# A gated cross-attention block on one core: a new opening for the first batch's mask, queries and keys

## The chip, the cores and the metric

The kernel runs on one core of one Trainium2 chip. The metric is the time of one execution in device microseconds (us). Engines: TensorE (PE) multiplies matrices, VectorE (DVE), ScalarE (ACT) and GpSimd (POOL) do elementwise work, SyncE (SP) issues most transfers. Transfers issued by SP stand in one queue, those issued by ACT in another; sixteen DMA engines serve both.

## What is computed

```python
def attention(query, key, value, mask, ...):      # 16 heads of 8, D = 128
    q = query @ qw.T + qb; k = key @ kw.T + kb; v = value @ vw.T + vb
    scores = einsum('bhqd,bhkd->bhqk', split(q) * DH ** -0.5, split(k))
    scores = where(mask[:, None] == 0, -1e9, scores)
    return merge(softmax(scores) @ split(v)) @ ow.T + ob

x = x + tanh(g_xattn[0]) * attention(layernorm(x), ctx, ctx, mask, ...)   # x: 16 x 56 x 128, ctx: 16 x 1500 x 128
x = x + tanh(g_ffn[0]) * mixture_of_experts(layernorm(x), ...)            # 8 experts, top 2, one shared
```

The mask has 16 x 56 x 1500 entries.

## The kernel before

One batch is one unit of work, and units are pipelined by hand: in unit k the program makes K of batch k+2, scores, their maxima and V of batch k+1, and transposed scores, exponentials and the product with V of batch k. Three buffers (`NB`) rotate for the context (`ctxT`), the score operand (`keys`) and V. Each engine has its own instruction stream, written in the order in which it runs; streams wait for each other on semaphores. `units` runs a unit function for k from -1 (on SP from -2) to 15, and calls a function of the table that it is given ahead of a unit. What stands ahead of `units` in each stream is the opening.

The score operand `keys[:, buffer, pair, :]` has 121 rows that one matmul contracts for a pair of heads: rows 0 to 63 are K as a high and a low fp16 part (rows r, r+4, ... for r = 0 to 3), rows 64 to 120 are the mask's additive term, one row per query, with a row of ones at row 96 (`ONEROW`), against which the running maximum is subtracted. The mask rows are the same for all eight pairs of heads. VectorE makes them once (`mask_add`, two halves of 750 keys on rows 0 to 63 and 64 to 127), and the sync queue copies them eight times into `keys` ("placing"), in four transfers a batch: 32 and 24 rows for either half, skipping the row of ones, which one transfer writes into all buffers at the start. K is placed in four transfers too, each 16 x 8 runs of 1500 values.

The opening loads x, the first context and the constants, normalises x (`dve_layer_norm`), turns it on TensorE (`turn_ln`, two halves), makes K of batch 0 (`pe_k`, three chunks) and all queries (`make_queries`, two halves), splits each into fp16 parts, and places them. `pe_any` and `dve_any` find the queries with no valid key. `pool_queries` makes the query operand `qrs` of a batch. The second stage of the opening (`load_second`, `load_third`) loads contexts 1 and 2, the next masks, places the queries of the later batches and loads the output weights (`ow_rows`, `o_bias`). Ahead of unit 0 TensorE folds V's bias into the output bias (`fold_bias`), which waits for these.

## Time and profile before

| | |
|---|---|
| time, median of 3 runs | 525.68 us (525.66 to 526.95) |
| profiled execution: its own time | 525.51 us |
| profiled execution: span | 523.7 us |
| PE busy | 473.9 us, 90% of the span |
| DVE busy | 399.2 us, 76% |
| ACT busy | 329.6 us, 63% |
| POOL busy | 160.5 us, 31% |
| moved by the DMA engines | 72.82 MB, 139 GB/s over the span |

The span is the time between the first and the last instruction that the profiler saw. The busy shares are means over the whole span: the opening (to about 57 us), the units of the loop (23 us each) and the mixture of experts at the end have different limits, so a stage is read by its own rows.

### The profile page before, as it was taken

The numbers are of one execution on the slowest core, as the hardware profiler recorded it, in microseconds if no ns is written. First come the engines' busy times: TensorE is split into PE (matmuls) and PEld (weight loads), VectorE is DVE, ScalarE is ACT, GpSimd is POOL, SyncE is SP. The second block draws the span as 40 slices with busy tenths as digits, with TensorE's granted clock in tenths as the row PEclk, the third lists the DMA queues.
The fourth block names the chain that finished last, engine by engine and source line by source line (L and its number), as shares of the span: only waits on it lengthen the run. The fifth ranks groups of instructions, "written<-read, shape, count | busy, mean of one in ns | idle before, by whom it ended". The sixth has DMA issues, their size and how long they took to land.

```text
span 523.7 us, 15766 instructions
## 1 busy us (share of the span) xinstructions
PE 473.9 (90%) x6779; PEld 351.7 (67%) x6779; DVE 399.2 (76%) x784; ACT 329.6 (63%) x422; POOL 160.5 (31%) x142
## 2 busy tenths in 40 slices
PE   1547699999999999999999999999989989999993
PEld 0214377867778686777768677786868856777772
DVE  7339477877877887787788787778867768888776
ACT  2311366666676666667666666766665788877872
POOL 4034326061532606153351615335194200000000
PEclk9959799999999999999999999999999999999998
DMA  5899986996979688796969869684500300221001
GB/s 165 179 254 195 245 193 134 250 200 165 192 173 202 147 184 177 165 199 169 207 134 197 173 162 197 173 171 105 120 3 2 84 2 25 57 73 51 3 1 35
DMA packets 39805, 72.82 MB, mean 139 GB/s; under 512 B 4638, under 2 KB 26271, under 8 KB 39736
## 3 DMA queue, kind: packets, MB, share of 16 engines
q1 hardware_dynamic: 38456, 70.90, 60.6%
q8 instruction: 53, 0.87, 0.8%
q10 hardware_dynamic: 1280, 0.92, 0.7%
q14 instruction: 16, 0.13, 0.1%
HBM read 24.28 MB, written 0.46 MB: 47 GB/s over the span
## 4 chain that ended last, share of the span: by engine, by line
PE 78%; DVE 7%; DMA 5%; ACT 3%; issue 3%; SPq 1%; POOL 1%; ACTq 0%; DVEq 0%
PE ring L342 16%; PE pv L382 16%; PE st L363 11%; PE ring L324 8%; PE ring L286 7%; PE st L858 7%; PE ring L911 6%; DMA ctxT<-in_ctx 4%; DVE max_part L536 2%; ACT v_ext L469 2%; DMA ident_h<-in_c_ident_h 2%; PE pv L911 2%; SPq L268 1%; PE ring L307 1%; PE ring L350 1%
## 5 line engine op out<-in xcount | busy, mean ns | idle before, releaser
L536 DVE TENSOR_REDUCE max_part<-ring 112x1 f32<-112x512 f32 (+1 forms) x384 | 244.9, 675 | 73.4 <-PE ring L342 73.2
L489 ACT ACTIVATE probs<-st 128x896 f32<-128x896 f32 x192 | 172.5, 916 | 73.5 <-PE st L363 71.4
L342 PE MATMUL ring<-keys,qrs 121*112 121x512 f16 (+1 forms) x384 | 149.7, 391 | 6.8 <-DVE max_part L536 3.3
L363 PEld LDWEIGHTS st<-qrs,keys 121*128 121x128 f16 (+1 forms) x1536 | 97.2, 102 | 29.5 <-issue 8.9
L363 PE MATMUL st<-qrs,keys 121*128 121x112 f16 (+1 forms) x1536 | 106.7, 213 | 1.0 <-ACT qrs L478 1.0
L382 PE MATMUL pv<-probs,v_ext 128*32 128x168 f32 (+3 forms) x3072 | 93.6, 262 | 0.1
L382 PEld LDWEIGHTS pv<-probs,v_ext 128*32 128x32 f32 (+1 forms) x3072 | 73.1, 109 | 21.7 <-issue 11.3
L342 PEld LDWEIGHTS ring<-keys,qrs 121*112 121x112 f16 x384 | 49.9, 130 | 41.7 <-DVE max_part L536 17.7
L614 POOL TENSOR_TENSOR k_hi<-k_raw,zero 128x512 f16<-128x512 f32 (+1 forms) x45 | 45.8, 1018 | 86.7 <-ACT k_raw L457 86.7
L286 PE MATMUL ring<-ctxT,w_qkv 128*128 128x512 f32 (+1 forms) x94 | 53.6, 656 | 13.7 <-DMA ctxT<-in_ctx 13.7
L324 PE MATMUL ring<-w_qkv,ctxT 128*128 128x128 f32 (+1 forms) x384 | 60.0, 278 | 1.7 <-ACT v_ext L469 0.5
L324 PEld LDWEIGHTS ring<-w_qkv,ctxT 128*128 128x128 f32 (+1 forms) x384 | 56.3, 188 | 6.4 <-ACT v_ext L469 4.4
L457 ACT ACTIVATE k_raw<-ring,biases 128x512 f32<-128x512 f32 (+1 forms) x45 | 30.5, 677 | 42.5 <-PE ring L286 40.6
L886 DVE TENSOR_TENSOR keys<-probs,keys 128x896 f16<-128x896 f32 (+2 forms) x44 | 40.3, 919 | 17.6 <-ACT keys L879 17.3
L617 POOL TENSOR_TENSOR k_lo<-k_raw,k_hi 128x512 f16<-128x512 f32 (+1 forms) x45 | 51.2, 1138 | 3.5
L635 POOL TENSOR_TENSOR attn<-sums,recip 128x112 f32<-128x112 f32 x15 | 6.3, 421 | 142.0 <-DVE recip L565 132.2
L869 ACT ACTIVATE probs<-st,up_bias 128x896 f32<-128x896 f32 (+2 forms) x44 | 38.2, 869 | 16.6 <-PE st L858 16.3
L858 PE MATMUL st<-keys 128*128 128x512 f16 (+1 forms) x216 | 47.7, 353 | 0.7 <-ACT probs L869 0.7
L469 ACT ACTIVATE v_ext<-ring 128x512 f32<-128x512 f32 (+1 forms) x48 | 27.1, 565 | 26.7 <-PE ring L324 26.7
L911 PE MATMUL ring<-keys 128*128 128x128 f16 x612 | 41.5, 219 | 1.6 <-DVE keys L886 1.6
L911 PEld LDWEIGHTS ring<-keys 128*128 128x128 f16 x612 | 36.5, 98 | 9.2 <-DVE keys L886 2.9
L626 POOL TENSOR_TENSOR qrs<-queries,any_key 121x896 f16<-121x896 f16 x16 | 30.2, 1887 | 22.5 <-DMA queries<-probs 22.5
(122 smaller groups left out, 352.0 us busy)
## 6 DMA issues: line engine op xcount, KB each, us to landing
ctxT<-in_ctx SPq DMA_DIRECT2D x16, 750.0 KB, 6.2
keys<-mask_add SPq DMA_DIRECT2D x32, 375.0 KB
keys<-k_hi SPq DMA_DIRECT2D x32, 375.0 KB, 6.3
keys<-k_lo SPq DMA_DIRECT2D x32, 375.0 KB, 7.3
keys<-mask_add SPq DMA_DIRECT2D x32, 281.2 KB
mask_raw<-in_mask SPq DMA_DIRECT2D x15, 375.0 KB, 3.5
up_w<-in_up_w SPq DMA_DIRECT2D x9, 256.0 KB, 2.9
down_w<-in_down_w SPq DMA_DIRECT2D x9, 256.0 KB, 3.2
```

Of the source, the lines that this page charges most:

```text
L286: nc.tensor.matmul((first_k[c] if known(k, -1) else misc)[:, 0:width(c)], w_qkv[:, 1, :], ctxT[:, w, chunk(c)], start=True, stop=True).the ...
L324: mm = nc.tensor.matmul(misc[0:m, i * P:(i + 1) * P], ctxT[:, buf(b, 1), j * P:j * P + m], w_qkv[:, 2, :], start=True, stop=True)
L342: nc.tensor.matmul(ring[0:QW, m % 2, 0:width(c)], qrs[0:ROWS, w, p, :, :].rearrange("r h q -> r (h q)"), keys[0:ROWS, w, p, chunk(c)], sta ...
L363: mm = nc.tensor.matmul(st[0:m, j % 2, p // 4, QW * (p % 4):QW * (p % 4 + 1)], keys[0:ROWS, u, p, j * P:j * P + m], qrs[0:ROWS, u, p, :, : ...
L382: mm = nc.tensor.matmul(pv[rows, last * HG * S:last * HG * S + n * S], v_ext[0:m, u, j, VW * h:VW * h + CW], probs[0:m, j % 4, S * h:S * ( ...
L489: nc.scalar.activation(probs[0:m, j % 4, :].rearrange("p (h c) -> p h c", h=2), st[0:m, j % 2, :, 0:HQ // 2], ACT.Exp).then_inc(s["exps_do ...
L536: nc.vector.tensor_reduce(max_part[:, p, c:c + 1], ring[0:QW, m % 2, 0:width(c)], AX.X, ALU.max).then_inc(s["max_read"], 1)
L614: nc.gpsimd.tensor_tensor(k_hi[:, chunk(c)], k_raw[:, chunk(c)], zero[:, :].to_broadcast([P, width(c)]), ALU.add).then_inc(s["k_hi_made"], 1)
L617: nc.gpsimd.tensor_tensor(k_lo[:, chunk(c)], k_raw[:, chunk(c)], k_hi[:, chunk(c)], ALU.subtract).then_inc(s["k_lo_made"], 1)
L858: mm = nc.tensor.matmul(st[:, n % 2, h, 0:cols], split_w[e][:, 0, w, c * P:(c + 1) * P], xn_p[:, x, 4 * P * h:4 * P * h + cols], start=(i ...
L886: nc.vector.tensor_tensor(hid[:, n % HR, 1, cols], hid_raw[n % 3][:, cols], hid[:, n % HR, 0, cols], ALU.subtract).then_inc(s["hid_lo_done ...
L911: mm = nc.tensor.matmul(down_banks[e % 2][t // 4][:, P * (t % 4):P * (t % 4 + 1)], hid[:, n % HR, x, P * t:P * (t + 1)], split_w[e][:, 1, ...
```

## The change

The first batch's mask no longer goes through `mask_add` and the sync queue. It is loaded in the layout of the mask rows (`first_mask`, 64 rows of 1500, into a part of `keys` that is free so early), VectorE makes the rows of pair 0 in place, and VectorE (pairs 1 and 2, then 3 to 5) and ScalarE (pairs 6 and 7) copy them to the other pairs. The row of ones is now a row of the mask: its entry is 0 and its factor 1 (`mask_scale`, one factor per row, in place of the constant -32768), so that one transfer places 64 rows, two transfers a batch instead of four, and the transfer that wrote the ones is gone. TensorE turns both halves of x and makes the first queries ahead of K; the identity for the maxima (`ident_h`) is waited for later. The first queries are issued by SP instead of ACT, ahead of the first keys, which are split into buffer 2 of `keys` and placed in three chunks, each with a semaphore of its own. Context 1 and mask 1 are issued once the first mask has landed, context 2 behind the first keys; the later queries follow the placement of mask 1, and the output weights stand behind batch 1's keys. TensorE makes the first chunk of batch 1's K ahead of unit -1.

```diff
+        first_hi, first_lo = keys[:, NB - 1, 0, :], keys[:, NB - 1, 1, :]
+        first_mask = keys[MROW:P, NB - 1, 2:4, :].rearrange("r p k -> r (p k)").bitcast(I32)
...
+        def sp_place_mask(sp, b):
...
+            for h in range(2):
+                sp.dma_start(keys[MROW:P, w, :, h * HK:(h + 1) * HK],
+                             mask_add[MROW * h:MROW * (h + 1), :].unsqueeze(1)
+                             .to_broadcast([MROW, PAIRS, HK])).then_inc(mask_placed[w], 16)
...
-                for h in range(2):
-                    for r0, r1 in ((0, QSPLIT), (QSPLIT + 1, NR)):
-                        sp.dma_start(keys[MROW + r0:MROW + r1, w, :, h * HK:(h + 1) * HK],
...
+                for c in range(NCH) if known(k, -1) else ():
+                    sp.wait_ge(s["k_lo_made"], c + 1)
+                    for r in range(4):
+                        sp.dma_start(keys[r:MROW:4, w, :, chunk(c)], (first_lo if r % 2 else first_hi)[:, chunk(c)])                            .then_inc(first_placed[c], 16)
...
+                if known(k, 0):
+                    pe.wait_ge(s["rows_spread"], 2)
+                    pe.wait_ge(s["rows_copied"], 1)
+                    pe.wait_ge(first_placed[0], 64)
...
-            nc.vector.tensor_scalar(mask_add[:, :], mask_raw[:, :], 0.0, -BIG,
+            nc.vector.tensor_scalar(mask_add[:, :], mask_raw[:, :], 0.0, mask_scale,
...
-            sp.wait_ge(s["ones_set"], 2)
-            sp.dma_start(keys[ONEROW:ONEROW + 1, :, :, :].rearrange("r u p k -> r (u p) k"),
-                         ones_row[:, :].unsqueeze(1).to_broadcast([1, NB * PAIRS, NK])).then_inc(s["ones_placed"], 16)
 
             def load_second():
+                sp.wait_ge(s["mask_loaded"], 16)
                 sp_load_ctx(sp, 1, 1)
                 sp_load_mask(sp, 1)
+                sp.wait_ge(s["q_hi_done"], 1)
+                sp_place_first_queries(sp, 0)
+                sp.wait_ge(s["q_split"], 1)
+                sp_place_first_queries(sp, 1)
+
+            def load_next():
+                sp.wait_ge(s["q_made"], 2)
+                sp_load_ctx(sp, 2, 2)
+                sp_place_mask(sp, (-1, -1 % NB, -1 // NB))
                 sp.wait_ge(s["q_split"], 2)
...
+            def load_output():
+                for c in range(NCH):
+                    sp.wait_ge(first_placed[c], 64)
                 sp.dma_start(ow_rows[:, :, :], d["ow"]).then_inc(s["consts_loaded"], 16)
                 sp.dma_start(o_bias[:, :], d["ob"].unsqueeze(0)).then_inc(s["consts_loaded"], 16)
-
-            def load_third():
-                sp_load_ctx(sp, 2, 2)
...
-            units(sp, sp_unit, {-1: load_second, 0: load_third, 2: load_ffn}, first=-2)
+            units(sp, sp_unit, {-2: load_second, -1: load_next, 0: load_output, 2: load_ffn}, first=-2)
...
+            act.wait_ge(s["mask_ready"], 1)
+            nc.scalar.activation(keys[MROW:ROWS, 0, COPIED:PAIRS, :],
+                                 keys[MROW:ROWS, 0, 0:1, :].to_broadcast([NR, PAIRS - COPIED, NK]),
+                                 ACT.Copy).then_inc(s["rows_copied"], 1)
...
-            pe.wait_ge(s["weights_loaded"], 32)
+            pe.wait_ge(s["weights_loaded"], 16)
             pe.wait_ge(s["qkv_loaded"], 32)
             turn_ln(0)
-            pe_k(pe, FIRST, 0)
-            pe_k(pe, FIRST, 1)
+            turn_ln(1)
             make_queries(0)
-            pe_k(pe, FIRST, 2)
-            turn_ln(1)
+            for c in range(NCH):
+                pe_k(pe, FIRST, c)
             make_queries(1)
-            pe_any(pe, FIRST)
-
-            def await_ones():
-                pe.wait_ge(s["ones_placed"], 16)
+
+            def second_k():
+                pe_k(pe, (-1, -1 % NB, -1 // NB), 0)
+                pe_any(pe, FIRST)
+                pe.wait_ge(s["ident_loaded"], 16)
...
+            def spread_mask(pairs):
+
+                dve.wait_ge(s["mask_ready"], 1)
+                n = len(pairs)
+                nc.vector.tensor_copy(keys[MROW:ROWS, 0, pairs[0]:pairs[-1] + 1, :],
+                                      keys[MROW:ROWS, 0, 0:1, :].to_broadcast([NR, n, NK])).then_inc(s["rows_spread"], 1)
```

On SP, from the last two placements of the first keys on (`k_hi`, `k_lo`) to the placement of mask 1, before:

```order
L268 DMA keys<-k_hi 16x8x1500
L268 DMA keys<-k_lo 16x8x1500
L240 DMA ctxT<-in_ctx 128x1500
L245 DMA mask_raw<-in_mask 128x750
L990 DMA queries<-probs 16x8x784 [waits s_q_split]
L990 DMA queries<-probs 16x8x784 x3
L992 DMA ow_rows<-in_ow 128x256
L993 DMA o_bias<-in_ob 1x128
L245 DMA mask_raw<-in_mask 128x750 [waits s_mask_abs_done,s_mask_ready]
L263 DMA keys<-mask_add 32x8x750
L263 DMA keys<-mask_add 24x8x750
```

Before these stood the ones row and the first mask's four placements; behind them follow the second half of mask 1, batch 1's keys, and only then context 2 (`ctxT`). On SP after the change, behind the twelve placements of the first keys:

```order
L257 DMA ctxT<-in_ctx 128x1500 [waits s_q_made]
L262 DMA mask_raw<-in_mask 128x750 [waits s_mask_abs_done,s_mask_ready]
L276 DMA keys<-mask_add 64x8x750 x2
L1031 DMA queries<-probs 16x8x784 [waits s_q_split]
L1031 DMA queries<-probs 16x8x784 x3
L296 DMA keys<-k_hi 16x8x1500 [waits s_k_lo_made]
L296 DMA keys<-k_lo 16x8x1500
L296 DMA keys<-k_hi 16x8x1500
L296 DMA keys<-k_lo 16x8x1500
L1037 DMA ow_rows<-in_ow 128x256 [waits s_first_placed2,s_first_placed1,s_first_placed0]
L1038 DMA o_bias<-in_ob 1x128
```

Context 2 moved from behind batch 1's keys to ahead of mask 1's placement, and the output weights from ahead of it to behind batch 1's keys.

On VectorE, from the end of the layer norm to the second half of the queries (`attn` is the raw queries, `probs` their fp16 parts), before:

```order
L511 TENSOR_SCALAR mask_add<-mask_raw 128x750 [waits s_mask_loaded,s_consts_loaded,s_qkv_loaded]
L513 TENSOR_REDUCE mask_abs<-mask_raw 128x1
L518 TENSOR_SCALAR any_row<-c_rows,mask_abs 128x56 [waits s_mask_abs_done]
L1168 SCALAR_TENSOR_TENSOR k_lo<-ring,biases,k_hi 128x512 [waits s_k_hi_made] x2
L1175 TENSOR_SCALAR attn<-st,biases 128x448 [waits s_q_made]
L1168 SCALAR_TENSOR_TENSOR k_lo<-pv,biases,k_hi 128x476 [waits s_k_hi_made]
L1182 TENSOR_TENSOR probs<-attn,probs 128x448 [waits s_q_hi_done]
L527 SCALAR_TENSOR_TENSOR any_key<-ring,halves 128x112 [waits s_any_spread,s_halves_loaded]
```

And after:

```order
L1236 TENSOR_SCALAR keys<-keys,biases 57x1500 [waits s_mask_loaded,s_consts_loaded,s_qkv_loaded]
L1216 TENSOR_SCALAR attn<-st,biases 128x448 [waits s_q_made]
L1232 COPY keys<-keys 57x3000 [waits s_mask_ready]
L1223 TENSOR_TENSOR probs<-attn,probs 128x448 [waits s_q_hi_done]
L1209 SCALAR_TENSOR_TENSOR keys<-ring,biases,keys 128x512 [waits s_k_hi_made] x2
L1244 TENSOR_REDUCE mask_abs<-keys 57x1 [waits s_abs_cleared]
L1209 SCALAR_TENSOR_TENSOR keys<-pv,biases,keys 128x476 [waits s_k_hi_made]
L1216 TENSOR_SCALAR attn<-st,biases 128x448 [waits s_q_made]
L1249 TENSOR_SCALAR any_row<-c_rows,mask_abs 128x56 [waits s_mask_abs_done]
L1232 COPY keys<-keys 57x4500 [waits s_mask_ready]
L561 SCALAR_TENSOR_TENSOR any_key<-st,halves 128x112 [waits s_any_spread,s_halves_loaded]
```

The first queries moved ahead of K's low parts, the reduction of the mask in between them, and the two copies that spread the mask are new.

## Rows read from the trace of the kernel before

**Rows 1.** Busy time by stage: us, busy (instructions) by engine, clock, DMA share.
```profile
core 0: us, PE busy (x) PEld busy (x) DVE busy (x) ACT busy (x) POOL busy (x), PEclk, DMA share, GB/s
...
53.80:57.35 3.55, 0.07 (x1) 0.00 (x0) 0.95 (x3) 0.77 (x1) 0.00 (x0) 0.64 0.97 374
57.35:81.27 23.92, 23.49 (x320) 17.05 (x320) 16.55 (x28) 14.48 (x19) 8.27 (x7) 0.91 0.78 172
```

**Rows 2.** Chain of waits, the opening's transfers: start, us, what it waited for.
```profile
2.95 8.68 DMA ident_h<-in_c_ident_h
...
23.42 9.35 DMA ctxT<-in_ctx
...
46.65 10.48 DMA ctxT<-in_ctx
```

**Rows 3.** Timeline of the opening: start, us, engine, line, operation.
```profile
8.98 1.88 DVE L968 TENSOR_SCALAR attn<-x_tok,ln_mv,ln_rstd 128x128 f32<-128x128 f32 x7
...
12.59 3.62 PE L286 MATMUL ring<-ctxT,w_qkv 128*128 128x512 f32 x4
...
34.69 1.06 PE L342 MATMUL ring<-keys,qrs 121*112 121x512 f16 x2
...
52.84 0.18 DVE L545 TENSOR_REDUCE neg_max<-max_part 112x8 f16<-112x24 f32 x1
```

**Rows 4.** Timeline of SP: when four transfers were issued, and for how long.
```profile
25.05 0.97 SPq L245 DMA_DIRECT2D mask_raw<-in_mask  x1
...
35.72 0.35 SPq L245 DMA_DIRECT2D mask_raw<-in_mask  x1
...
42.95 0.58 SPq L268 DMA_DIRECT2D keys<-k_hi  x1
...
45.67 0.93 SPq L268 DMA_DIRECT2D keys<-k_lo  x1
```

**Rows 5.** Transfers by short stretches in order of issue: KB, us to landing.
```profile
mask_raw<-in_mask SPq DMA_DIRECT2D x1, 375.0 KB, 9.2
...
L990 SPq DMA_DIRECT2D queries<-probs x4: 542/598/599, 26.1 to 27.9; - x4
...
queries<-probs SPq DMA_DIRECT2D x1, 196.0 KB, 10.2
...
mask_raw<-in_mask SPq DMA_DIRECT2D x1, 375.0 KB, 4.0
...
keys<-k_hi SPq DMA_DIRECT2D x1, 375.0 KB, 6.2
...
keys<-k_lo SPq DMA_DIRECT2D x1, 375.0 KB, 9.7
...
k_hi<-k_lo SPq DMA_DIRECT2D x1, 2.2 KB, 1.7
```

**Rows 6.** Opening's instructions by shape: count, busy us, mean ns, idle before.
```profile
L513 DVE TENSOR_REDUCE mask_abs<-mask_raw 128x1 f32<-128x750 int32 x3 | 2.8, 927 | 0.0
...
L511 DVE TENSOR_SCALAR mask_add<-mask_raw 128x750 f16<-128x750 int32 x3 | 1.6, 549 | 9.8 <-DMA mask_raw<-in_mask 9.8
...
L1168 DVE SCALAR_TENSOR_TENSOR k_lo<-ring,biases,k_hi 128x512 f16<-128x512 f32 x2 | 1.5, 750 | 3.1 <-ACT k_hi L1043 3.1
...
L1175 DVE TENSOR_SCALAR attn<-st,biases 128x448 f32<-128x448 f32 x2 | 1.3, 674 | 0.0
...
L626 POOL TENSOR_TENSOR qrs<-queries,any_key 121x896 f16<-121x896 f16 x16 | 30.2, 1887 | 22.5 <-DMA queries<-probs 22.5
```

**Rows 7.** Around the start of unit 3: last keys' issue and landing, first score.
```profile
115.66 0.88 SPq L268 DMA_DIRECT2D keys<-k_lo  x1
...
keys<-k_lo SPq DMA_DIRECT2D x1, 375.0 KB, 8.0
...
128.33 0.13 PEld L342 LDWEIGHTS ring<-keys,qrs 121*112 121x112 f16 x1 [0.84 <-issue]
...
128.79 1.30 DVE L536 TENSOR_REDUCE max_part<-ring 112x1 f32<-112x512 f32 x2 [0.73 <-PE ring L342]
```

117 lines of the change are left out of this document (70 added, 47 removed).

## The prediction

> **What bounds the kernel now.** I read the stages first, then the chain of waits, then the timeline of the opening with the transfers. From 57 us on one batch follows the other with TensorE always busy: the stage 57.35 to 81.27 is 23.92 us long and PE is busy for 23.49 of it [rows 1]. Nothing that the change does there can give time back; it can only cost some. The opening is different. The chain of waits holds three stretches that end with a transfer: TensorE's first transpose waits until 11.63 us (2.95 + 8.68) for `ident_h`; it then waits for batch 1's context, issued at 23.42 and landed 9.35 later at 32.77; and for batch 2's context, issued at 46.65 and landed 10.48 later at 57.13 [rows 2]. In the stage before that last landing, 53.80 to 57.35, PE is busy 0.07 us while the DMA engines are 97% busy [rows 1]. So the contexts are late because they stand at the end of a full queue: from the first mask placement on, the sync queue's transfers run one behind the other without a gap, and batch 2's context is the last of them. The question is how long that queue is afterwards, when it starts, and what stands last in it.
>
> **What a transfer takes.** Landing is issue plus the time to landing. Batch 1's keys: the first of four lands at 42.95 + 6.2 = 49.15, the last at 45.67 + 9.7 = 55.37 [rows 4, 5], so 6.2 for three, 2.07 each of 375 KB. The context behind them: 57.13 − 55.37 = 1.8. Batch 1's mask: 25.05 + 9.2 = 34.25, 1.5 after the context at 32.77 [rows 2, 4, 5]. The four later queries of 196 KB: the last lands at 27.9 + 10.2 = 38.1, so 3.85 for four, 0.96 each. After them `ow_rows`, `o_bias` and the next mask land by 35.72 + 4.0 = 39.72, 1.6 together: I take 1.2 for the mask and 0.6 for the other two. Mask placement of batch 1 runs from 39.72 to 49.15 − 2.07 = 47.1: 7.4 us.
>
> **The change, part by part.**
>
> *Removed from the queue:* the placement of the first mask (as long as batch 1's, 7.4 us) and the ones row. The rows are spread on VectorE and ScalarE instead.
>
> *TensorE's start.* `ident_h` is no longer waited for, so the first transpose follows the first normalised tile. Seven tiles take 1.88 us from 8.98 [rows 3], so TensorE starts at about 9.3, 2.3 earlier, and is through with both halves at 11.2. The query product comes before K now. Two K chunks took 3.62 in this stretch [rows 3], some 1.7 each, and 448 columns instead of 512 make 1.5: queries at 12.75, K chunks at 14.45, 16.15 and 17.8.
>
> *VectorE and ScalarE up to the first issue.* Scaling (0.674 [rows 6]) ends at 13.5, ScalarE's half of the split at 14.1. Then VectorE spreads pairs 1 and 2: 3000 fp16 elements per row. No such copy is in the trace. The nearest single-source operation from SBUF to SBUF is `mask_add`, 0.549 us for 750; the slow bound is the reduction of the same 750 elements, 0.927 [rows 6]. Less some 0.15 that I allow for what each pays once, that is 0.53 and 1.03 ns an element, so 1.75 or 3.25 us. I take the first, since it is the same kind of operation. The spread ends at 15.2, the split at 15.8, the low part of the first keys (0.750 [rows 6]) at 16.6. The Trainium skill, "VectorE: DVE Perf Modes", section "The perf-mode tier table", gives a 16-bit copy within SBUF four elements a cycle. By an estimate from it the spread would take 0.95 us and the forecast would be 0.5 us earlier; no row here shows that rate.
>
> *The sync queue.* It issues the high queries from 14.15, the low ones from 15.85, at 0.6 each (as the later queries, 0.598 [rows 5]), and the first keys from 17.05. Twelve transfers of 128 KB replace four of 375 KB. Their cost each is unknown: by bytes from the queries' 0.96 it is 0.63, from the keys' 2.07 it is 0.71; the upper bound is 0.96, if the 128 runs count and not their length. I take 0.75, a little over what bytes give. A small lone transfer lands 1.7 us after its issue [rows 5], so the first lands at 17.05 + 1.7 + 0.6 = 19.35, the last 11 × 0.75 later at 27.6. Issuing (0.6 each) keeps ahead. The low part of chunk 2 waits behind the 1500-element reduction (twice 0.927 less one start, 1.7) and is ready at 20.2, before its turn at 22.
>
> *The queue behind them.* Batch 2's context, now ahead, 1.8: 29.4. Mask 1.2: 30.6. Placement in two transfers of 64 rows instead of 32 and 24: between 7.4 as now and 7.4 × 64/56 = 8.5 by bytes; I take 7.8, nearer to the first, since two transfers replace four: 38.4. Later queries 3.9: 42.3. Keys of batch 1, 8.2: 50.5; their values are ready near 33, so the queue is what they wait for. Then `ow_rows` and `o_bias`, 0.6: 51.1. On the placement the Trainium skill, "DMA: Bandwidth & Descriptors", section "Why a DMA increments its semaphore by 16 and not by 1", says that a copy uses the largest number of engines up to 16 that divides its slowest dimensions. By that, 24 rows go on 12 engines and 32 or 64 rows on 16, the busiest engine has 64 runs before and after, and the longer placement costs nothing: 0.4 less than the sum has. No row here counts engines.
>
> *What batch 1's unit waits for.* The first scores need the spread rows, the first key chunk (21.6) and the scaled queries, which GpSimd makes after `any_key`. VectorE gets there after the reduction, the second scaling and the second spread (4500 elements, 2.5 us): about 23.6, GpSimd's 1.9 [rows 6] later 25.5. Before, the first score started at 34.69 and the last maximum was merged at 52.84, 18.15 later [rows 3]. So this unit's scores now end near 43.7, and its row of maxima near 45.
>
> *What is late next.* Not the context any more: batch 2's landed at 29.4. TensorE folds the value bias before unit 0, and that waits for `ow_rows` and `o_bias`, which moved to the end of the queue: 51.1. For the fold, VectorE's addition and the handovers I allow 1.0: unit 0 starts at 52.1 instead of 57.38. TensorE idles before it about as now (about 6 us instead of 3.5), so I leave the clock granted in unit 0 as it is, 0.91 [rows 1]. From there on the order is the same.
>
> *The loop.* Each batch's placement may grow by 1.1 us at most. The last keys of a batch land at 115.66 + 8.0 = 123.66, and the first score that reads them loads at 128.33: 4.7 us of cover [rows 7]. `mask_add` takes its factor from SBUF now; at the reduction's rate it would grow by 0.4, against 0.73 us that VectorE idles before the next maximum [rows 7]. Both cost nothing; without that cover it would be 0.4 a batch.
>
> **Sum.** 57.38 − 52.1 = 5.3 us. The profiled execution took 525.51 us (span 523.7 and 1.8 around it), 0.17 below the median of 525.68, so I predict 520.2 us, 1.0% faster.
>
> **Rivals.** *The spread is slow and the key chunks too.* At the slow bounds the first issue is 1.5 us later and twelve chunks at 0.96 take 2.5 longer; the placement by bytes adds 0.7. All the queue behind moves: 522.5 to 524.9. For it: neither a copy nor a 128 KB transfer is in the trace. Against: the neighbours on both sides. Chance 0.09.
>
> *The queue is no bound.* If the transfers overlapped more, unit 0 would follow the maxima at 45: another 6 to 7 us, 513 to 515. Against it speaks that the engines were 97% busy before unit 0. Chance 0.04.
>
> *Slower: a transfer's time doesn't shrink with its bytes.* If each of the twelve took 2.07, as a quarter of the keys does with the same 128 runs, the first keys would take 24.8 instead of 9.0 and unit 0 would start at 68: 536. It decides from 1.19 us each, (9.0 + 5.3) / 12. Against: four transfers with 128 runs and half the bytes took 0.96 each. Chance 0.04. The Trainium skill, "DMA: Bandwidth & Descriptors", section "Anatomy of one DMA", gives a copy 2.0 us plus its bytes at 436 GB/s. Paid one after the other that would be an estimated 2.3 each and a slower kernel. The trace disagrees for transfers that queue: 0.96 with 196 KB.
>
> *No change.* The time gained is given back in unit 0, by a lower clock after the longer wait or because masks and keys of batch 2 come late in their turn. They would have to cost 3.7 us of 23.9; batch 2's transfers keep their place relative to unit 0. Chance 0.03.
>
> **Numbers.** The forecast's own case holds 0.80. Its range is made by the bounds: chunks at 0.63, the placement at 7.4 and a quicker spread make 518.0; half of the first rival makes 522.8. Faster by over 0.3% (1.6 us, about what this measurement can tell from no change) is the forecast, the second rival and the first one: 0.92 with something taken off for its tail; within 0.3%: 0.04; slower: 0.04.
>
> **What would show it.** First transpose near 9.3; no placement from `mask_add` before 25 us; twelve key transfers landing between 19 and 28, some 0.75 apart; batch 2's context at 29 to 30; first score near 25.5; TensorE idle from about 45 to 51, and that wait ended by `ow_rows` or `o_bias`, no longer by `ctxT`; unit 0 from 52 on; units of 23.0 us as before. I am wrong if the wait before unit 0 ends with something else, if the spread takes over 3 us, if the keys of batch 1 land long before 50, or if the units of the loop change.

## The result and the profile after

The changed kernel took 521.67 us (median of 4 runs, 521.40 to 521.86) against 525.67 for the kernel before beside it: a ratio of 0.9918, with a 95% interval of 0.9901 to 0.9935. Forecast were 520.2 us and a range of 518.0 to 522.8, so the time is in the range and 1.5 us above the forecast. The profiled execution has a span of 520.0 us against 523.7, which is 3.7 us less.

Three stretches of the changed kernel, with the columns of [rows 1]: the wait before unit 0, unit 0, and 4 us behind the loop.

```profile
45.70:53.27 7.57, 1.01 (x4) 0.36 (x5) 1.18 (x3) 0.87 (x1) 0.00 (x0) 0.50 1.04 275
53.27:76.25 22.98, 22.58 (x320) 16.38 (x320) 16.43 (x28) 14.49 (x19) 8.23 (x7) 0.95 0.79 167
...
421.00:425.00 4.00, 4.00 (x37) 3.16 (x35) 2.89 (x14) 2.40 (x5) 0.00 (x0) 0.59 0.00 0
```

The first K product of unit 13, the last unit that makes K, in TensorE's timelines of the kernel before and of the changed kernel:

```profile
357.39 1.13 PE L286 MATMUL ring<-ctxT,w_qkv 128*128 128x512 f32 x2
...
353.17 1.12 PE L312 MATMUL ring<-ctxT,w_qkv 128*128 128x512 f32 x2
```

Unit 0 starts at 53.27 instead of 57.38, 4.1 us earlier. It takes 22.98 us instead of 23.82 (57.38 to 81.20), which gives 0.8 more. From unit 1 to unit 13 it is 276.92 us (76.25 to 353.17) instead of 276.19 (81.20 to 357.39), and from there to the end 166.83 instead of 166.31. These two take 0.7 and 0.5 back: 4.1 + 0.8 − 0.7 − 0.5 makes the 3.7. The row from 421 to 425 us shows part of the last loss. The granted clock was 0.59 there, a mixture of its two levels of 1.2 and 2.4 GHz; in the profile before, the same work ran at 1.00.

The opening in the chain of waits (start, us, what it waited for), in the pieces that answer to [rows 2]:

```profile
9.66 1.92 PE st L1137 x7
...
23.96 2.15 DVE mask_add L545
...
35.33 2.68 SPq L1031
...
43.02 8.78 DMA o_bias<-in_ob
51.84 1.01 PE pv L1163 x4
52.86 0.42 issue
53.27 2.05 PE ring L312 x2
```

`ident_h` and both contexts are gone from the chain. TensorE starts at 9.66 instead of 11.68, and the wait before unit 0 now ends with `o_bias`, at 43.02 + 8.78 = 51.80. Before that stands a full queue, as the sync queue's own timeline shows (issue, us spent on issuing, what):

```profile
14.78 2.58 SPq L221 DMA_DIRECT2D queries<-probs  x4
17.41 7.70 SPq L292 DMA_DIRECT2D keys<-keys  x12
25.15 0.60 SPq L257 DMA_DIRECT2D ctxT<-in_ctx  x1
27.05 0.33 SPq L262 DMA_DIRECT2D mask_raw<-in_mask  x1
27.42 1.32 SPq L276 DMA_DIRECT2D keys<-mask_add  x2
28.78 9.23 SPq L1031 DMA_DIRECT2D queries<-probs  x4
...
40.80 1.06 SPq L296 DMA_DIRECT2D keys<-k_lo  x1
```

SP itself is held up by the full queue: four transfers of queries were issued in 2.58 us at 14.78 and in 9.23 at 28.78.

How long these transfers took from issue to landing, for the twelve of the first keys and the two of the placement (ns of issuing, first and last issue):

```profile
L292 SPq DMA_DIRECT2D keys<-keys x12: 597/600/611, 17.4 to 24.5; - x12
...
DMA to landing us min/median/max: 2.4/2.5/2.6
L276 SPq DMA_DIRECT2D keys<-mask_add x2: 635/637/639, 27.4 to 28.1; - x2
...
DMA to landing us min/median/max: 8.9/10.3/11.8
```

And the three lone ones, from the view of transfers by short stretches (KB, us to landing):

```profile
ctxT<-in_ctx SPq DMA_DIRECT2D x1, 750.0 KB, 4.9
mask_raw<-in_mask SPq DMA_DIRECT2D x1, 375.0 KB, 5.3
keys<-k_lo SPq DMA_DIRECT2D x1, 375.0 KB, 10.7
```

Issue plus landing gives the course of the queue; the last of the later queries, issued at 35.33, landed 9.6 later.

| what has landed | forecast | measured |
|---|---|---|
| first of twelve key transfers | 19.35 | 19.8 |
| last of them | 27.6 | 27.0 |
| batch 2's context | 29.4 | 30.05 |
| the mask issued ahead of the placement (batch 2's) | 30.6 | 32.35 |
| placement of batch 1's mask | 38.4 | 39.9 |
| later queries | 42.3 | 44.9 |
| keys of batch 1 | 50.5 | 51.5 |
| `o_bias` | 51.1 | 51.8 |
| unit 0 starts | 52.1 | 53.27 |

The spread of the first mask, in VectorE's groups by shape (busy us, mean ns):

```profile
L1232 DVE COPY keys<-keys 57x4500 f16<-57x4500 f16 x1 | 2.5, 2494 | 0.0
L1232 DVE COPY keys<-keys 57x3000 f16<-57x3000 f16 x1 | 0.9, 939 | 0.0
```

The second mask's preparation on VectorE, and GpSimd's operation beside it, in the timeline:

```profile
23.87 2.24 DVE L545 TENSOR_SCALAR mask_add<-mask_raw,biases 128x750 f16<-128x750 int32 x1
...
23.60 2.10 POOL L660 TENSOR_TENSOR qrs<-queries,any_key 121x896 f16<-121x896 f16 x1 [16.66 <-DVE any_key L561]
```

The first spread takes 0.94 us where 1.75 was taken; 1.5 times the elements take 2.49, 2.7 times as long. `mask_add` takes 2.24 us, against 0.60 in the units behind, and it begins 0.27 after GpSimd's `qrs` and ends 0.4 after it.

### The profile page after: what moved, and what is told of

It reads as the page before. It is cut to its first block, busy times and chain, and to the rows that moved or that the text cites. A ratio compares the mean times of both kernels' runs of the same rounds, so it can differ in the third digit from the quotient of the medians.

```text
span 520.0 us, 15739 instructions
## 1 busy us (share of the span) xinstructions
PE 475.7 (91%) x6779; PEld 353.0 (68%) x6779; DVE 404.6 (78%) x786; ACT 332.4 (64%) x423; POOL 161.0 (31%) x142
## 2 busy tenths in 40 slices
DMA packets 41465, 74.28 MB, mean 143 GB/s; under 512 B 4339, under 2 KB 28532, under 8 KB 41397
## 4 chain that ended last, share of the span: by engine, by line
PE 78%; DVE 9%; ACT 4%; issue 3%; SPq 3%; DMA 3%; DVEq 0%
PE pv L416 16%; PE ring L376 16%; PE st L397 11%; PE ring L350 9%; PE st L892 7%; PE ring L312 6%; PE ring L945 6%; DVE max_part L570 2%; ACT v_ext L503 2%; SPq L1031 2%; DMA o_bias<-in_ob 2%; PE pv L945 2%; PE ring L333 1%; PE ring L384 1%; DVE sums L592 1%
## 5 line engine op out<-in xcount | busy, mean ns | idle before, releaser
L920 DVE TENSOR_TENSOR keys<-probs,keys 128x896 f16<-128x896 f32 (+2 forms) x44 | 40.4, 919 | 17.7 <-ACT keys L913 17.4
L312 PE MATMUL ring<-ctxT,w_qkv 128*128 128x512 f32 (+1 forms) x94 | 51.8, 636 | 0.4 <-issue 0.4
L903 ACT ACTIVATE probs<-st,up_bias 128x896 f32<-128x896 f32 (+2 forms) x44 | 38.3, 869 | 17.7 <-PE st L892 17.4
L945 PEld LDWEIGHTS ring<-keys 128*128 128x128 f16 x612 | 37.6, 100 | 9.1 <-DVE keys L920 2.5
L913 ACT ACTIVATE keys<-probs 128x896 f16<-128x896 f32 (+2 forms) x44 | 35.8, 814 | 1.4
```

The source lines that it names most:

```text
L312: nc.tensor.matmul((first_k[c] if known(k, -1) else misc)[:, 0:width(c)], w_qkv[:, 1, :], ctxT[:, w, chunk(c)], start=True, stop=True).the ...
L920: nc.vector.tensor_tensor(hid[:, n % HR, 1, cols], hid_raw[n % 3][:, cols], hid[:, n % HR, 0, cols], ALU.subtract).then_inc(s["hid_lo_done ...
L945: mm = nc.tensor.matmul(down_banks[e % 2][t // 4][:, P * (t % 4):P * (t % 4 + 1)], hid[:, n % HR, x, P * t:P * (t + 1)], split_w[e][:, 1, ...
```

## The experiments

Two theories stood against each other at the start. The first is that of the forecast: what ends before unit 0 is the length of one queue, so each byte put into it or each later start moves unit 0. The second: single waits (the fold of the output weights, the second mask, the first chunks) set unit 0, and the queue's length matters little. The times of several chips are compared by the ratio to the kernel before on the same chip, which took 525.7 to 527.2 us. The starts are those of one profiled execution each. Of two kernels there are two: the changed one started unit 0 at 53.27 and 53.43, and the one with the early output weights moved 214 and 227 GB/s from 19.4 to 51.5 us and started its first score of unit 0 at 52.01 and 51.18. So a difference of less than 1 us between two starts is not read as an effect.

| kernel | ratio, 95% interval | unit 0's first K | unit 1's first K |
|---|---|---|---|
| before | 1 | 57.38 | 81.20 |
| changed | 0.9918, 0.9901 to 0.9935 | 53.27 | 76.25 |
| changed, again | 0.9892, 0.9877 to 0.9907 | 53.43 | 76.62 |
| 64-row placement alone | 1.0043, 1.0023 to 1.0063 | 59.20 | 83.73 |
| first keys whole | 0.9930, 0.9903 to 0.9957 | 53.28 | 77.62 |
| two more loads | 0.9994, 0.9976 to 1.0011 | 56.89 | 80.54 |
| late start | 0.9950, 0.9926 to 0.9973 | 55.12 | 79.33 |
| context earlier | 0.9897, 0.9877 to 0.9917 | 52.72 | 76.19 |
| `mask_add` first | 0.9898, 0.9876 to 0.9920 | 53.86 | 76.83 |
| output weights early | 0.9883, 0.9853 to 0.9913 | 46.40 | 74.28 |
| the same again | 0.9877, 0.9855 to 0.9898 | 46.41 | 74.30 |
| and one queue order | 0.9871, 0.9856 to 0.9886 | 46.34 | 74.16 |
| and context by ScalarE, first | 0.9886, 0.9866 to 0.9906 | 48.35 | 74.93 |
| and context by ScalarE, second | 0.9848, 0.9823 to 0.9873 | 48.28 | 74.66 |

**The 64-row placement alone**, in the kernel before, in place of its four transfers of 32 and 24 rows and without the ones row:

```diff
+                for h in range(2):
+                    sp.dma_start(keys[MROW:P, w, :, h * HK:(h + 1) * HK],
+                                 mask_add[MROW * h:MROW * (h + 1), :].unsqueeze(1)
+                                 .to_broadcast([MROW, PAIRS, HK])).then_inc(mask_placed[w], 16)
...
```

> The kernel before, with one part of the change alone: 64 rows in two transfers instead of 32 and 24 in four, the ones as a row of the mask, and no transfer of ones at the start. By bytes each placement in the opening takes 8.5 to 8.9 us instead of 7.4, there are two of them ahead of the context that unit 0 waits for, so unit 0 starts near 59.8 instead of 57.4 and the time is about 528. If a copy of 24 rows keeps only part of the engines busy and the busiest engine has the same work before and after, the placements take as long as now and the time stays at 525.5. Both: units of the loop stay at 23.0 us.

The ratio makes 2.3 us more (0.0043 × 525.7). In the chain of this kernel the context that unit 0 waits for comes 1.8 later than in [rows 2], at 58.95 instead of 57.13:

```profile
49.78 9.17 DMA ctxT<-in_ctx
```

Two placements of 188 KB more each move 0.38 MB; at the 205 GB/s that the kernel before moved from 38.0 to 47.5 us this is 1.9 us. But the edit did more than add bytes, so this agreement does not show the cause. Without the ones row (70 KB, issued at 2.78 before) `ident_h` landed at 2.94 + 6.2 = 9.1 instead of 11.63, the first transpose started at 9.51 instead of 11.68, and the first keys were issued at 17.24 instead of 19.79. And batch 1's mask landed at 25.56 + 10.98 = 36.54 instead of 34.25; around this time the queue moved less than before (SyncE windows, first of the kernel before, then of this one):

```profile
31.00:38.00 7.00, 0.52 1.05 267
38.00:47.50 9.50, 1.00 1.03 205
...
31.00:38.00 7.00, 0.50 0.88 223
38.00:47.50 9.50, 0.99 0.95 190
```

Behind it, batch 2's mask had landed at 38.10 + 4.1 = 42.2 and the placement of batch 1's at 39.16 + 10.7 = 49.86, 7.7 us against the 7.4 of before. So the whole loss arose up to 36.54, with the first placement, which the changed kernel no longer has. That the placement of 64 rows costs something in the kernel before is shown; how much of it is bytes and how much the emptier queue is open. In the changed kernel the placement took 39.9 − 32.35 = 7.6 us between the landings.

**The first keys as four whole transfers**, as before, and not in three chunks:

```diff
-                for c in range(NCH) if known(k, -1) else ():
-                    sp.wait_ge(s["k_lo_made"], c + 1)
+                if known(k, -1):
+                    sp.wait_ge(s["k_lo_made"], NCH)
                     for r in range(4):
-                        sp.dma_start(keys[r:MROW:4, w, :, chunk(c)], (first_lo if r % 2 else first_hi)[:, chunk(c)])
+                        sp.dma_start(keys[r:MROW:4, w, :, :], (first_lo if r % 2 else first_hi)[:, :])\
...
```

> The changed kernel with the first keys placed whole, in four transfers after the last chunk, instead of twelve in three chunks. If the queue behind them is what unit 0 waits for, the keys end near 28.5 to 29.5 instead of 27.1, everything behind moves by 1 to 1.5 us, and the time is 522.7 to 523.2, although the first scores start 3 to 4 us later. If the early start of the scores is what the chunks are worth, the time is 3 to 4 us longer, 525 or more.

The first keys landed at 21.63 + 7.21 = 28.84 instead of 27.0, as expected, and the first score started 3.2 later, at 28.98. But unit 0 starts at 53.28, the same, since `o_bias` ends the wait here too (43.00 + 8.80 in its chain). The 1 to 1.5 us that the theory of the queue expected did not come, so keys that are late by themselves need not move the end; what made up for them is open. The ratio is 0.0012 above that of the changed kernel, 0.6 us, inside both intervals (0.0038 above its repeat, where the intervals still overlap). The chunks bring nothing to unit 0's start that can be measured. In the profiled execution unit 0 took 24.3 us, with a granted clock of 0.65 from 55 to 60 us where the changed kernel had 0.93; that is a difference of one execution, and what makes the clock rise later is open.

**Two more loads behind batch 2's context**, of 750 KB each, whose data nothing uses:

```diff
                 sp_load_ctx(sp, 2, 2)
+                for i in range(2):
+                    sp.dma_start(spare[:, i, :], d["ctx"][0, :, :]).then_inc(s["spare_loaded"], 16)
```

> The changed kernel with two more loads of a context (750 KB each, into a tile that nothing reads) behind the load of context 2. If the opening is as long as the sync queue, each costs its 1.8 us: unit 0 starts near 56.9 and the time is 525.3. If the transfers of the opening have room beside each other, or TensorE's own work sets unit 0's start, it stays at 521.7.

`o_bias` lands at 55.41 instead of 51.80, and unit 0 starts at 56.89, 3.62 later, as a full queue demands; two loads at 1.8 each make 3.6:

```profile
45.43 9.98 DMA o_bias<-in_ob
56.89 2.05 PE ring L313 x2
```

The time rises by 0.0076 of 525.7, 4.0 us. This also gives the price of a load behind another of its kind: the two landed at 25.9 + 6.0 = 31.9 and 26.4 + 7.3 = 33.7, 1.8 apart. Batch 2's context itself landed 30.05 − 27.0 = 3.1 behind the last of the first keys in the changed kernel, and 1.8 behind the last keys of batch 1 in the kernel before. There it had been issued 8.7 us ahead of that landing (46.65 and 55.37), here 1.9 (25.15 and 27.0). The load of the same size that was issued at 10.48, with only a mask behind it, took 4.2 from issue to landing, and this one 4.9; so it stood too short a time in the queue to be hidden there.

**A late start.** TensorE waits for `ident_h` at its start:

```diff
+            pe.wait_ge(s["ident_loaded"], 16)
...
                     mm = nc.tensor.transpose(st[:, 0, h, i * P:(i + 1) * P], xn[:, t, :], ident)
```

> The changed kernel with one edit: TensorE waits at its start for the identity matrix of 16 bits that ScalarE's queue loads last (it lands at about 11.0 us), as the first product of the kernel before did; the first transposes then start at about 11.0 instead of 9.66. Theory (all of the opening hangs on the first transposes, through the queries, the first keys and one full queue): the first keys are issued at about 18.7 instead of 17.41, and unit 0 starts 1.0 to 1.4 us later, 54.3 to 54.7, the ratio at 0.993 to 0.995. Rival (the end of the opening hangs on bytes that don't wait for the queries, the mask and context loads): unit 0 moves by less than 0.4 us.

```profile
11.12 1.73 PE L1137 MATMUL st<-c_f,attn 128*128 128x128 f32 x7 [11.12 <-DVE attn L1002]
...
55.12 2.05 PE L312 MATMUL ring<-ctxT,w_qkv 128*128 128x512 f32 x2 [0.42 <-issue]
```

The first transpose starts 1.46 later, the first keys are issued 1.4 later (18.81) and unit 0 starts 1.85 later (1.7 against the repeat), somewhat more than the 1.0 to 1.4 expected. The end of the opening hangs on the first transposes; the rival, with a move of less than 0.4, falls.

**The context ahead of the first keys:**

```diff
                 sp_place_first_queries(sp, 1)
-
-            def load_next():
                 sp.wait_ge(s["q_made"], 2)
                 sp_load_ctx(sp, 2, 2)
+
+            def load_next():
```

`load_next` runs behind the issue of the first keys, so what stands ahead of its first line is issued ahead of them.

> The changed kernel with one edit: the load of the second context tile is issued right behind the first queries, ahead of the twelve first-key transfers instead of behind them. Theory (the transfers ahead of unit 0 are one queue; it loses time while the twelve short transfers are bound by their issue, 0.65 us each, and where it ran empty ahead of the context load, 27.1 to 29.4 us): the context load fills these gaps, the first keys land up to 3 us later, all that stands behind them is issued up to 2 us earlier, unit 0 starts 1 to 2 us earlier (about 51.5 to 52.3 against 53.27), the ratio to the kernel before about 0.988 to 0.990. Rival (the wait for the second mask's preparation on VectorE sets when the placement starts, whatever the queue holds): the second mask is still issued at 27.05, unit 0 starts within 0.4 us of 53.27, and the ratio stays at 0.992. Second rival: the first scores start later by the 3 us and their maxima become what unit 0 waits for: unit 0 at 53.3 or later.

My theory of gaps missed. `o_bias` lands at 42.84 + 8.41 = 51.25, half a microsecond earlier, unit 0 starts at 52.72, 0.6 earlier (0.7 against the repeat) instead of 1 to 2, and the ratio equals that of the changed kernel beside it (0.9897 and 0.9892). The stretch that I had taken for an empty queue was none, as the SyncE windows of the changed kernel show (us, granted clock, DMA share, GB/s):

```profile
20.00:27.00 7.00, 0.61 0.78 196
27.00:30.00 3.00, 0.50 0.86 286
32.50:45.70 13.20, 0.99 1.08 204
```

From 27 to 30 us the context itself was moving, at 286 GB/s. And while the twelve short transfers ran, the engines' share was 0.78, but they moved 196 GB/s, about as many as later at a share of 1.08. So there was next to nothing to fill. A share under 1 was no free room here; the GB/s say it.

**`mask_add` ahead of `any_key`:**

```diff
+            if k != -1:
...
+            dve.wait_ge(s["mask_loaded"], 32)
+            nc.vector.tensor_scalar(mask_add[:, :], mask_raw[:, :], 0.0, mask_scale,
+                                    ALU.is_equal, ALU.mult).then_inc(s["mask_ready"], 1)
             dve_any(dve, FIRST)
             split_queries(1)
```

> The changed kernel with one edit: VectorE converts the second mask (mask_add) ahead of the any_key operation that releases GpSimd's first multiplication of queries, instead of behind it. Theory (mask_add took 2.24 us instead of 0.60 since GpSimd's qrs ran beside it, and the late mask held back the queue): mask_add takes 0.60, GpSimd's qrs starts 0.6 us later and takes about 1.9 instead of 2.10, the second mask is issued at about 25.8 instead of 27.05, the queue no longer runs empty, and unit 0 starts 0.8 to 1.3 us earlier (52.0 to 52.5). Rival (mask_add is slow for another reason, such as the DMA writing into SBUF at that time or its first use of the operand): it takes over 1.5 us at the new place too and unit 0 moves by less than 0.3. Second rival (the queue's bytes alone set the end): mask_add takes 0.60 and unit 0 moves by less than 0.3.

```profile
23.28 0.61 DVE L1255 TENSOR_SCALAR mask_add<-mask_raw,biases 128x750 f16<-128x750 int32 x1
23.80 0.27 DVE L562 SCALAR_TENSOR_TENSOR any_key<-st,halves 128x112 f16<-128x112 f32 x1
23.99 0.61 DVE L1224 TENSOR_TENSOR probs<-attn,probs 128x448 f16<-128x448 f32 x1
24.52 0.93 DVE L548 TENSOR_REDUCE mask_abs<-mask_raw 128x1 f32<-128x750 int32 x1
25.48 0.92 DVE L553 TENSOR_SCALAR any_row<-c_rows,mask_abs 128x56 f16<-128x56 f32 x1
...
24.25 2.10 POOL L661 TENSOR_TENSOR qrs<-queries,any_key 121x896 f16<-121x896 f16 x1 [17.30 <-DVE any_key L562]
```

Away from GpSimd's `qrs` the same `mask_add` takes 0.61 us, and now the other tensor-scalar operation, `any_row`, stands beside `qrs` and takes 0.92 instead of 0.25. The reduction beside it keeps its time, and so does `probs`, which had started 0.26 before it. That `mask_add` was held up by GpSimd's operation is shown. But the next mask and the placement, issued from 25.82 on instead of 27.05, bring nothing: unit 0 starts at 53.86, 0.4 to 0.6 later, and the ratio is that of the changed kernel's repeat on the same chip. This is nearest to the second rival, by which the bytes set the end: the 1.6 us of `mask_add` cost nothing. Why unit 0 is rather later than the same is open; the queue moved 213 GB/s from 19.4 to 51.5 us, against 221 and 217 in the changed kernel.

**The output weights early.** `ow_rows` and `o_bias` are loaded ahead of the first queries, with a semaphore of their own:

```diff
+                sp.dma_start(ow_rows[:, :, :], d["ow"]).then_inc(s["output_loaded"], 16)
+                sp.dma_start(o_bias[:, :], d["ob"].unsqueeze(0)).then_inc(s["output_loaded"], 16)
                 sp.wait_ge(s["q_hi_done"], 1)
                 sp_place_first_queries(sp, 0)
...
-                sp.dma_start(ow_rows[:, :, :], d["ow"]).then_inc(s["consts_loaded"], 16)
-                sp.dma_start(o_bias[:, :], d["ob"].unsqueeze(0)).then_inc(s["consts_loaded"], 16)
```

> The changed kernel with the output weights and bias loaded ahead of the first queries, while the queue is empty. If unit 0 waits for them, it now makes its first K near 46 and waits for batch 1's keys instead, which land near 51: first score near 51.5 instead of 55.1, time 518 to 519. If the wait for them only covers a wait of the same length for something else, the time stays within 1 us of 521.7.

TensorE's timeline shows what is late next when `o_bias` is no longer the last (in brackets the idle time ahead and what ended it):

```profile
44.52 0.48 PE L384 MATMUL ring<-ident_h,neg_max 112*1 112x112 f16 x5 [0.96 <-DVE neg_max L579]
...
46.40 2.05 PE L312 MATMUL ring<-ctxT,w_qkv 128*128 128x512 f32 x2 [0.67 <-issue]
52.01 0.65 PE L376 MATMUL ring<-keys,qrs 121*112 121x512 f16 x1 [3.56 <-DMA keys<-k_lo]
```

Unit 0's first K product now follows the maxima at 46.4, 6.9 us earlier, but its first score still waits for batch 1's keys. It starts at 52.01 instead of 55.11, and unit 1 is 2.0 earlier (2.3 against the repeat). This kernel was run again, beside the first try of the context on ScalarE's queue:

> The kernel with the output weights loaded ahead of the first queries once more, unaltered, beside the next kernel on one chip. Theory: unit 0's first K product starts at about 46.4 as soon as the maxima are done, its first score at 52.0 with the last keys of batch 1, unit 1 at 74.3, and the ratio to the kernel before is 0.985 to 0.989, under the changed kernel's 0.989 to 0.992. Rival (the gain of that edit was the scatter of the runs): a ratio of 0.990 or more.

The repeat gives 0.9877 and the same starts of units 0 and 1; its last keys landed at 40.56 + 10.38 = 50.94 and its first score started at 51.18, 0.8 earlier than in the first execution. Against the changed kernel (0.9918 and 0.9892) the gain is 0.1 to 0.4%, 0.5 to 2 us. The start of unit 1 shows it in both profiles, while the intervals of the ratios overlap. Against the kernel before it is clear.

**One queue order.** To the early output weights, the context is added behind the first chunk, and the later queries ahead of the second mask:

```diff
                 for c in range(NCH) if known(k, -1) else ():
...
+                    if c == 0:
+                        sp.wait_ge(s["q_made"], 2)
+                        sp_load_ctx(sp, 2, 2)
...
             def load_next():
-                sp.wait_ge(s["q_made"], 2)
-                sp_load_ctx(sp, 2, 2)
-                sp_place_mask(sp, (-1, -1 % NB, -1 // NB))
...
+                sp_place_mask(sp, (-1, -1 % NB, -1 // NB))
```

> The kernel with the output weights loaded early (ow_rows and o_bias ahead of the first queries) and two more moves in the sync queue: the second context tile is issued behind the first chunk of the first keys, and the later queries ahead of the second mask and its placement. Theory (one queue without gaps is what unit 0's first score waits for): the queue stays full from 20 us on, the last keys of batch 1 land about 2 us earlier than in the kernel with the early output weights alone (49.5 to 50.5 against 52.0), and the time is 1 to 2 us under that kernel's, at a ratio of about 0.984 to 0.987 to the kernel before. Rival (the queue moves bytes at one rate and the gaps were not lost time): last keys within 0.5 us of 52.0, ratio 0.988.

The keys of batch 1 land at 37.99 + 13.53 = 51.52, against 40.47 + 11.30 = 51.77 and 50.94 without the new order: the rival holds. From 27 to 30 us only short transfers inside SBUF were landing now, with more of them waiting than before (SyncE windows of this kernel):

```profile
20.00:27.00 7.00, 0.56 1.00 227
27.00:30.00 3.00, 0.50 1.13 195
```

They moved 195 GB/s at a share of 1.13, where the changed kernel moved 196 GB/s at 0.78. The fuller queue raised the share and not the rate.

**The context by ScalarE's queue**, twice, on top of the early output weights:

```diff
             split_queries(0)
+            act.wait_ge(s["q_made"], 2)
+            nc.scalar.dma_start(ctxT[:, 2, :], d["ctx"][2:3, :, :].rearrange("b d k -> d (b k)")).then_inc(ctx_loaded[2], 16)
             for c in range(NCH):
                 first_k_hi(c)
```

The second try has the two new lines behind the loop instead, and `mask_add` ahead of `any_key` as above.

> The kernel with the output weights loaded early, and the second context tile's load given from the sync queue to ScalarE's queue, issued at about 15 us ahead of the first keys' activations. Theory (the transfers inside SBUF move about 195 GB/s whatever else stands in their queue, and the context load from memory is a rate of its own): the context load runs beside the first keys' transfers, takes no turn in their queue, and everything behind is 2.5 to 3.5 us earlier: last keys of batch 1 at about 49 instead of 52.0, unit 0's first score there too, unit 1 at 71.5 to 72.5 and a ratio of 0.981 to 0.983. Rival (the 16 DMA engines share one total, whichever queue issues): the first keys land 2 to 3 us later beside the context load, the last keys still land at 51.5 to 52.2, unit 1 stays within 0.4 us of 74.3 and the ratio at 0.986 to 0.988.

This run doesn't tell the two apart. ScalarE waited for the second query product until 17.2 and issued the load at 17.23 ahead of its key activations; so the first keys were issued at 19.12, 1.7 late, and the second mask at 29.45. The load was over before the first key landed, and all behind was later by its own start. From 27 to 30 us the DMA engines moved only 77 GB/s: here, with the context out of the way, the wait for `mask_add` did leave the queue nearly empty. The second try holds nothing back:

> The kernel with the output weights loaded early, the second context tile's load issued by ScalarE's queue behind the three first-key activations (about 17.4 us) instead of ahead of them, and VectorE's mask_add ahead of any_key. Unlike the run before it this one holds nothing back: the first keys are issued at 17.4 and the second mask at about 25.8. Theory of one shared total (the transfers of both queues share about 195 to 230 GB/s): the first keys land up to 3 us later beside the context load, the last keys of batch 1 land at 50.7 to 51.7, unit 1 starts within 0.5 us of 74.3, ratio 0.985 to 0.988. Rival (the sync queue's transfers inside SBUF are held to 195 GB/s by their own queue and the context load adds to it): first keys as before to 27.2, last keys of batch 1 at 48 to 49, unit 1 at 71.5 to 72.5, ratio 0.981 to 0.984.

The context, issued at 18.20 and landed 5.2 later, ran beside the first keys. Most of these now took 5.8 us to land instead of 2.5:

```profile
L292 SPq DMA_DIRECT2D keys<-keys x12: 596/608/857, 17.5 to 24.9; - x12
...
DMA to landing us min/median/max: 2.4/5.8/6.1
```

And in TensorE's timeline unit 0's first score:

```profile
51.46 0.65 PE L376 MATMUL ring<-keys,qrs 121*112 121x512 f16 x1 [1.14 <-DMA keys<-k_lo]
```

Batch 1's keys land at 40.03 + 11.19 = 51.22, between those of the two executions without the edit, and unit 1 starts at 74.66. While context and first keys moved together, the rate was this (SyncE windows):

```profile
20.00:27.00 7.00, 0.71 1.03 236
```

With the same context in SP's queue among the first keys it was 227 in the same 7 us (the one queue order above), and 234 with the context ahead of them. So the second queue added next to no rate: the theory of one shared total holds, and the queue of the forecast is really the transfers of all queues together. The ratio, 0.9848, is the lowest of all, but its five runs go from 517.63 to 522.03, its profiled execution was the slowest of them, and its interval overlaps that of the early output weights (0.9855 to 0.9898). That the context by ScalarE adds something is open.

**The changed kernel again:**

> The changed kernel once more, unaltered. Theory (the 1.4 us that its profile lost behind the loop against the profile before came from the granted clock, which fell to half at about 421 to 424 us in that execution only): where the clock stays whole there, the stretch from unit 1's first K product to the end is about 442.5 us as in the kernel before instead of 443.75, and the ratio stays at 0.990 to 0.993. Rival (the drop belongs to the changed kernel): the clock falls at the same place again.

From 421 to 425 us the granted clock is 1.00 this time, and from unit 1 to the end it takes 519.7 − 76.62 = 443.1 us, against 443.75 in the first profile and 442.5 before (523.7 − 81.20). So the drop accounts for some 0.65 of the 1.25 us, not for all as the theory had it, and the ratio, 0.9892, lies just under the expected 0.990. Five of the fourteen profiles show a drop there (0.84 to 0.91 from 412 to 432 us: the changed kernel, two more loads, context earlier, `mask_add` first, and the second context by ScalarE), nine show 1.00, the repeat and the kernel before among them. So it does not come with every execution of the changed kernel; what sets it off is open. Over all profiles that stretch is 442.1 to 445.5 us long, so one execution can differ by 3 us behind the opening. Medians over several runs are what to go by.

## Why the prediction was right

**The bound.** Right: the wait before unit 0 ends with the last transfer of a full queue. In the kernel before, this queue began with the placement of the first mask (timeline of SP):

```profile
12.88 4.79 SPq L263 DMA_DIRECT2D keys<-mask_add  x4
```

From there it is 44.25 us to the landing of batch 2's context at 57.13 [rows 2]; in the changed kernel it is 34.39 from the first keys at 17.41 to `o_bias` at 51.80. The queue is 9.86 shorter and begins 4.53 later, and the fold, which was not on the path before, costs 1.22 more (1.47 against the 0.25 from landing to first product): 4.11 us, what unit 0 gained. Two more loads lengthened it by what they cost, and a later start of the whole opening moved its end; other orders of the same transfers moved unit 0 by 0.4 to 0.7 either way, no more than executions of one kernel can differ. What the removal of the first placement, the largest part, is worth by itself was not run.

From the last of the first keys to the last keys of batch 1 the forecast had 22.9 us (27.6 to 50.5), measured are 24.5 (27.0 to 51.5). In this stretch land 4909 KB of 1024 bytes (context 750, mask 375, placement 1500, queries 784, keys 1500), so 5.03 MB: 205 GB/s, the same as in the kernel before from 38.0 to 47.5 us. The 22.9 would have needed 220. Bytes over that one rate would have been the better sum.

The reading that the queue before had no gap is not quite right: from 42 to 44 us it moved 153 GB/s at a share of 0.85, while SP waited until 42.95 for GpSimd's low part of the keys. This lies inside the 7.4 us that the forecast took for a placement.

**What is late next.** Right: TensorE stands still from 45.70 until `o_bias` has landed at 51.80, and with the early output weights unit 1 starts 2.0 to 2.3 us earlier, with the keys of batch 1 close behind. First score and row of maxima came at 25.80 and 45.04, against 25.5 and 45.

**The start.** First transposes at 9.66 against 9.3, first keys issued at 17.41 against 17.05. The late start shows that such a difference goes on to unit 0 (1.46 became 1.7 to 1.85). That the first transpose no longer waits for `ident_h` has a second reason: in the 64-row placement alone, where that wait still stood, it started at 9.51 because the ones row was gone.

**The spread.** 1.75 us were taken for the first part and 0.94 measured; 2.5 for the second and 2.49 measured. The Trainium skill, "VectorE: DVE Perf Modes", section "The perf-mode tier table", gave the estimate of 0.95 for the first; the trace agrees for that one (0.94), and the second ran at little more than half that rate. The 0.8 us of the first were not gained: the sync queue issued the four first queries from 14.78 to 17.36 without a pause and the keys right behind them, so the spread had left the path, and what counted was that the queries were 0.6 later than the forecast's 14.15: the transposes started 0.36 late, and the query product took 1.86 us instead of 1.5.

**The twelve transfers.** 0.75 each were taken, measured are 0.65 (17.4 to 24.5 in eleven steps, at the same time to landing). That is SP's spacing of issues, and 128 KB at 196 GB/s take about as long, so which of the two sets it is not shown. The two rivals about them (0.96 each, or 2.07 each) fall. The 2.0 us that the forecast quoted from the Trainium skill, "DMA: Bandwidth & Descriptors", section "Anatomy of one DMA", are given there for transfers that GpSimd issues; these are issued by SP, and 0.65 apart nothing of that size is paid one after the other.

**The terms that were too small.** "Batch 2's context, now ahead, 1.8", "Mask 1.2" and "Later queries 3.9": between the landings they took 3.1, 2.3 and 5.0. The 1.8 was read where the context had long stood in the queue; here it had not (see the two more loads). The 1.2 was no reading: the landings left 1.6 for mask and output weights together, and 1.2 and 0.6 were taken. These three make 3.5 us and are what put unit 0 late. The keys of batch 1, 8.2 forecast and 6.6 measured (44.9 to 51.5), gave 1.6 back: the landings overlap, so a gap between two landings is no exact price of one transfer. So the sum is better than its terms, and that is luck in part. The forecast's upper bound of 522.8 is 0.25 higher than its own working gives: half of the first rival's 4.7 us on top of 520.2 is 522.55.

**The placement.** 7.8 forecast, 7.6 measured between the landings. The forecast's price by bytes, 8.5, came from the 7.4 with its gap; at 205 GB/s the 1500 KB take 7.5. By the rule of the Trainium skill, "DMA: Bandwidth & Descriptors", section "Why a DMA increments its semaphore by 16 and not by 1", the forecast's estimate was that the longer placement costs nothing. The 7.6 us fit either, and the 64-row placement alone changed more than this, so no run here decides between them.

**The fold.** 1.0 was allowed and 1.47 measured (51.80 to 53.27): the product at the lower clock level takes 1.01 and the handover 0.42.

**Unit 0 and the loop.** Unit 0's clock was taken as it was, 0.91, and it was 0.95, while unit 0 took 0.8 us less. Most units of the loop are 23.0 us as before, with `mask_add` at 0.60 instead of 0.55 hidden; in 13 of the 14 profiles one or two of the twelve from unit 1 to unit 13 are longer, up to 24.2, and why is open. Those twelve took 276.92 and 276.97 us in the changed kernel, 276.19 in the kernel before, and 276.05 and 277.09 in the two executions with the early output weights. From unit 13 on it was 166.83 and 166.11, before 166.31. So the 1.25 us that the profiled execution lost behind unit 0 lie within what executions of one kernel differ by. The time of 521.67 is 1.5 above the forecast: the gain was 4.0 by the medians, of which 1.2 of the 5.3 was missed at unit 0, and the rest is what unit 0 gained and the stretch behind it lost.

## What to carry to other kernels

Where an opening is one long queue of transfers, add up the bytes of all queues between the first issue and the last landing that a unit waits for, and divide by the rate at which the full queue moves. Here reordering them, filling what looked like gaps, or issuing from another engine changed little; two more loads, a later start of all of it, and a unit that no longer depended on the last transfer changed much. When a late transfer is moved off the end, look for a small one that now stands last: loading 128 KB and 0.5 KB of output weights early brought unit 1 forward by more than any other order did. And read the GB/s beside the engines' busy share before calling a stretch free.

## What the runs showed of the hardware that was not expected

Two of VectorE's tensor-scalar operations that started behind GpSimd's `qrs` were held up by it: `mask_add` took 2.24 us instead of 0.61 and `any_row` 0.92 instead of 0.25, each ending with or just after it, while a reduction (0.93) that started behind it and a tensor-tensor operation from fp32 (0.61) that started 0.26 before it kept their times. GpSimd's own operation took 2.10 instead of the usual 1.89 at those places.

The copy of one row to several pairs took 0.94 us for 57x3000 and 2.49 for 57x4500 elements; why the longer one is slower per element was not tried.

Twelve transfers of 128 KB moved 196 GB/s at a DMA share of 0.78; the larger ones behind moved 204 at 1.08.
